# First attention's slots: GpSimd waits for the buffers of four slots at once, at every fourth slot, in place of at every slot

## What is computed

```python
feat = (x @ W).reshape(n_nodes, H, D)
e = leaky_relu(el[src] + er[dst], 0.2)
ex = exp(e - segment_max(e, dst)[dst])
denom = segment_sum(ex, dst)
out = segment_sum((ex / denom[dst])[:, :, None] * feat[src], dst)
```

## Time and profile before

| | |
|---|---|
| median of 3 runs | 3279.8 us |
| profiled execution: span from its first to its last instruction | 3272.4 us |
| PE busy | 2624.1 us, 80% |
| DVE busy | 2317.7 us, 71% |
| ACT busy | 1279.7 us, 39% |
| POOL busy | 1066.1 us, 33% |
| first attention's slots | about 1556 to 2793 us |

### The profile page before, as it was taken

One profiled execution on the slowest core, in us unless ns is written; L12 is line 12 of the kernel. 1 busy time (PEld: TensorE's weight loads), 2 busy tenths in 40 slices (PEclk: granted clock), 3 DMA queues, 4 the chain that ended last, 5 costly groups with the idle time before them and its releaser, 6 DMA issues.

```text
span 3272.4 us, 51000 instructions
## 1 busy us (share of the span) xinstructions
PE 2624.1 (80%) x17803; PEld 1952.4 (60%) x17803; DVE 2317.7 (71%) x3106; ACT 1279.7 (39%) x3089; POOL 1066.1 (33%) x1299
## 2 busy tenths in 40 slices
PE   5777777999899997285888888777677677876999
PEld 3666664545455554265777777555555555674888
DVE  7999997796334443288788787966666666785786
ACT  7888884020001112001444444444544454503443
POOL 3000000111102225530566666666666665003000
PEclk8999999999899998597999999899988999967999
DMA  4444446434477872031677766666666666061543
GB/s 134 183 181 177 167 182 240 123 113 134 143 262 255 261 253 89 15 106 53 181 194 193 198 190 184 179 186 186 184 184 189 184 184 190 12 200 54 158 155 112
DMA packets 316172, 537.23 MB, mean 164 GB/s; under 512 B 114066, under 2 KB 219044, under 8 KB 315668
## 3 DMA queue, kind: packets, MB, share of 16 engines
q1 hardware_dynamic: 244724, 308.43, 28.8%
q0 software_dynamic: 71200, 225.54, 24.7%
HBM read 419.84 MB, written 115.21 MB: 164 GB/s over the span
## 4 chain that ended last, share of the span: by engine, by line
PE 53%; DVE 28%; issue 7%; another core or an unknown queue 5%; ACT 5%; DMA 1%; POOL 1%; DVEq 0%; ACTq 0%; SPq 0%; POOLq 0%
PE ps L1718 20%; PE ps L1499 14%; PE ps L1706 8%; DVE a L590 8%; PE ps L1635 4%; DVE a L585 3%; DVE a L586 3%; PE ps L1405 2%; DVE a L1165 2%; DVE a L836 2%; ACT oht L1370 2%; DVE a L862 1%; ACT oh L1372 1%; PE ps L1633 1%
## 5 line engine op out<-in xcount | busy, mean ns | idle before, releaser
L1718 PE MATMUL ps<-a,oh 128*128 128x260 f32 x2008 | 508.8, 408 | 133.2 <-DVE a L1177 55.1
L1827 POOL DMA_INDIRECT a<-t,mid x502 | 486.7, 969 | 376.9 <-PE ps L1718 140.3
L1370 ACT ACTIVATE oht<-iota,mid 128x128 f32<-128x128 f32 x830 | 333.3, 402 | 627.0 <-PE ps L1718 396.4
L1499 PE MATMUL ps<-a 128*128 128x512 f32 x1200 | 555.4, 602 | 13.4 <-DVE a L769 13.4
L1718 PEld LDWEIGHTS ps<-a,oh 128*128 128x128 f32 x2008 | 389.7, 201 | 233.7 <-ACT oh L1372 97.3
L1165 DVE TENSOR_TENSOR a<-a,ps 128x520 f32 x415 | 286.3, 690 | 290.3 <-PE ps L1718 193.5
L1718 PE MATMUL ps<-wts,oh 128*128 128x260 f32 x1312 | 342.8, 416 | 115.2 <-DVE wts L1177 42.7
L1466 PE MATMUL ps<-a 128*128 128x200 bf16 x1568 | 320.4, 255 | 108.7 <-issue 51.1
L1827 POOL DMA_INDIRECT wts<-t,mid x328 | 313.5, 956 | 178.8 <-issue 82.9
L1718 PEld LDWEIGHTS ps<-wts,oh 128*128 128x128 f32 x1312 | 261.4, 206 | 184.4 <-ACT oh L1372 77.6
L1499 PEld LDWEIGHTS ps<-a 128*128 128x128 f32 x1200 | 218.8, 192 | 221.8 <-issue 215.4
(11 more groups left out here) (329 smaller groups left out, 3910.5 us busy)
## 6 DMA issues: line engine op xcount, KB each, us to landing
a<-at_d SPq DMA_DIRECT2D x60, 1280.0 KB, 6.1
at_d<-a SPq DMA_DIRECT2D x49, 800.0 KB, 3.3
mt_d<-a SPq DMA_DIRECT2D x49, 800.0 KB, 4.9
a<-mt_d SPq DMA_DIRECT2D x30, 1280.0 KB, 6.1
a<-trlo_d SPq DMA_DIRECT2D x49, 512.0 KB
ot_d<-a SPq DMA_DIRECT2D x49, 320.0 KB, 5.9
a<-ot_d SPq DMA_DIRECT2D x49, 256.0 KB, 3.3
a<-t,mid POOLq DMA_INDIRECT x502
```

The lines of the kernel that those rows point to most:

```text
L1370: e.activation(oht[:, k, :], iota[:, :], ACT.Abs, bias=ndl[:, k, s:s + 1]).then_inc(*own.inc())
L1499: m = e.matmul(acc[f].rearrange("p (x d) -> p x d", x=8), X[:, hi, P * f:P * (f + 1)], a, start=(hi == 0), stop=end, skip_group_check=True)
L1718: t = e.matmul(pbig[b][:, 512 * u:512 * u + 260], oh[:, so, k, :], hrows[2 * r + k][:, 260 * u:260 * (u + 1)], start=(k == 0), stop=(k == 1))
L1827: e.indirect_dma_start(out=hrows[2 * r + k], out_offset=None, in_=t2, in_offset=bass.IndirectOffsetOnAxis(ap=srci[:, k, s:s + 1], axis=0)) ...
```

## The change

GpSimd's wait moves from every slot to every fourth (s = 10, 14, 18, ...), and it then asks for the buffers of all four slots that follow: `head_mm` at s - 6 in place of s - 9. The last group's wait is cut at 405. The three slots behind it have no wait of their own.

The two waits of the first stage on a register's value change in form: the value goes through a register operation (the larger of it and 1) into a register that is kept, in place of `e.snap`.

```diff
@@ scalar @@
             ereg = [e.alloc_register(f"ae{i}") for i in range(4)]
+            ends = e.alloc_register("pair_end")
             e.wait_ge(*V("regs"))
...
-                e.wait_ge(slot_done, e.snap(ereg[p % 4], min_val=1, max_val=S))
+                e.reg_alu(ends, ereg[p % 4], 1, ALU.max)
+                e.wait_ge(slot_done, ends)
@@ tensor @@
             breg, freg = [], []
+            free = e.alloc_register("free_at")
...
-                    e.wait_ge(window_free, e.snap(freg[s // 8 % 4], donate=True, min_val=1, max_val=NPAIR + 8))
+                    e.reg_alu(free, freg[s // 8 % 4], 1, ALU.max)
+                    e.wait_ge(window_free, free)
@@ gpsimd @@
             def gather_heads(s):
                 r = s % NR
-                if s >= NR:
-                    e.wait_ge(head_mm, s - NR + 1)
+                if s >= NR and (s - NR) % 4 == 0:
+                    e.wait_ge(head_mm, min(s - NR + 4, NS - NR))
                 for k in range(2):
```

## The result

The changed kernel took 3413.03 us (median of 4 runs, 3398.04 to 3420.16); the kernel before took 3279.59 us beside it (3279.08 to 3279.99). The ratio is 1.040, 95% interval 1.037 to 1.043: slower by 133 us, where 50 were forecast. The profiled span went from 3272.4 to 3406.9 us, 134.5 more.

A forecast was written before the change was run, and what follows sets the result against it. While gathers are under way, their DMA queue was taken to hold back TensorE's counts, so the engines wait in rounds. Terms of 12 + 38 + 0 + 0 = 50 us gave 3330 us, range 3257 to 3392.

The forecast's parts named there:

- the register operations: First stage, two register waits: VectorE hides the added operations, 0 us; 17 us were that cover gone.
- the two kinds of round in the first part: First stretch, 1605 to 2047 us: rounds of eight gathers take 11.94 or 14.54 us, half of each assumed.
- the last part's single rounds: Last stretch, 2108 to 2763 us: a round of eight gathers takes 11.94 us, 2.985 per slot against 2.931.
- the sum of the last stretch: 2108 to 2763 us, 223.5 slots: the fourth count adds 0.2 us per round, 12 us; ends 1 and 114.
- the first stretch: 1605 to 2047 us, 145 slots: 3.31 us per slot against 3.048, 38 us; ends -9 and +85.
- The long round: First stretch: the fourth slot is computed only after the release, 11.74 + 2.8 = 14.54 us, 3.635 per slot.
- the upper end: First stretch: TensorE's clock falling from 0.98 to 0.91 costs 30 us at most, left out of the sum.
- what the DMA queue needs for the gathers: Long stretches of the first attention: the queue's draining, about 1.47 us per gather, sets the round and delays TensorE's counts.
- Much slower (3400 us): Rival: first stretch +85, clock +30 (part within that), last stretch 35, together 120 to 150 us; chance 0.16.
- Longer rounds save the stops: Rival, not slower, 3262 us: first stretch -16 us, last stretch a small gain, -2 us; chance 0.20.
- Rounds of eight below 11.5 us: Sign in the trace after: rounds of eight gathers ending before 11.5 us would show the forecast wrong.
- No difference: Rival, 3283 us: first stretch finds its four counts (-9), last pays for the fourth (+12), +3 us; chance 0.14.

The follow-up runs named there:

- e1: The changed kernel with GpSimd's wait put back before every slot, the register operations kept: 3281.43 us, ratio 1.002 to the kernel before.
- e9: The changed kernel itself, unaltered, run on another chip where the kernel before took 2976 us: ratio 1.0031 to it.
- e3: The changed kernel with waits at every slot and half of each gather's bytes (half rows): 3278.81 us, ratio 1.0013 to the kernel before.
- e4: The changed kernel, waits still in groups of four, with half of each gather's bytes (half rows): 3389.47 us, ratio 1.035 to the kernel before.
- e15: The changed kernel's groups of four plus a wait for the landing of the previous group's last gather: ratio 1.109 to the kernel before.
- e14: The changed kernel with waits at every slot and a memset of one column behind each gather: ratio 1.0007 to the kernel before.
- e18: The changed kernel with waits in groups of two slots in place of four: 3313.07 us, ratio 1.011 to the kernel before.

## Why the prediction was wrong

**Right:** slower, GpSimd's waits fewer and longer, ended by the last of four counts; rows still in time (3.6 us idle ahead of L1177); the first stage unchanged (VectorE 397.05 against 397.09 us of 400, and ScalarE's last clearing of PSUM starts at 529.2 us, before at 531.5), with the register operations put at 0 and 7.6 us in e1; the two kinds of round in the first part; the last part's single rounds, 11.8 us against 11.94 forecast. That the long and the short rounds of the first part come half and half was taken for want of a row, and was luck. One reading was loose without harm: VectorE is the gathered rows' first reader, but TensorE reads them too, scaled.

**The step that failed** is the sum of the last stretch, "every round becomes one of eight, and ends with the fourth count". Eight rounds were of sixteen, and two pairs nearly so. The forecast let TensorE finish four slots in a round of eight gathers; counted in the trace it finished five (180 slots done at 2186.52, 185 at 2198.41, 190 at 2208.40). So surplus counts pile up until the next group's wait is met at once; GpSimd then issues 20 us without a stop, and for the second half of it nobody gets a count. The ten double rounds take 285 us for 80 slots, 3.56 each against 2.93: 50 us, where the whole term was 12. The 36 single rounds together cost 2. The forecast held the length of a burst fixed by the code; it is fixed only from below.

**A term too small:** the first stretch, 38 forecast, 66 measured. The long round was put at 14.54 us, from one catch-up of 2.8 us; the long rounds take 15.7 on average and up to 18.5. The slot after the release also waits for ScalarE's and VectorE's work and runs at the low clock: 3.80 us for eight matmuls at 1883.94 in the changed kernel, where 1.84 were assumed. I gave the clock to the upper end only; at 0.84 in the last part and 0.94 in the first it belonged in the sum. How much it adds by itself, no run separates.

**A term left out:** the slots ahead of the first part, 16 us. The sum has nothing for them, and the first wait alone, which asks for three slots more, idles 9.3 us longer; on the other kind of chip it is the greater part of what the change costs (8.1 us in e9).

**A mechanism that was wrong:** that the round is "what the DMA queue needs for the gathers". e3 and e4 refute it as far as bytes go. The Trainium skill (DMA: Bandwidth & Descriptors, on the anatomy of a GpSimd-issued DMA) was set aside in the forecast because the rounds contradict it; by its 2.0 us plus bytes over 436 GB/s a gather's bytes move in less than the 1.25 us of its issue, and slots would come at 2.5 us; both are estimates. e9's trace, on the other kind of chip, shows just those 2.50 us. e15 shows a landing later than the rule's 2.6 us for 266 KB, 3.44 us behind the issue's end (the row at 2405.38), with seven other gathers just ahead of it. On the chip of the result something else held the slots.

A sign of that something was visible in the trace of the kernel before, outside the stretch I read. Between 1285 and 1365 us GpSimd issues 64 small gathers (4 KB each), one each 1.25 us, 3 GB/s in all. TensorE's work of that time does not wait for them. Stretches of the kernel before, then TensorE's instructions and one of VectorE's there:

```profile
1320.00:1340.00 20.00, 2.03 (x7) 0.73 (x7) 0.99 (x1) 0.00 (x0) 15.13 (x17) 0.50 0.08 3
...
1380.00:1400.00 20.00, 18.24 (x196) 16.20 (x194) 20.00 (x24) 0.00 (x0) 0.00 (x0) 1.00 0.18 50
```

```profile
1361.62 0.33 PE L1633 MATMUL ps<-small,yt 100*128 100x200 bf16 x1 [2.47 <-issue]
1364.42 0.33 PE L1635 MATMUL ps<-tbl,yt 128*128 128x200 bf16 x1 [2.47 <-issue]
...
1372.12 0.32 PE L1635 MATMUL ps<-tbl,yt 128*128 128x200 bf16 x1 [0.38 <-issue]
...
1372.84 0.99 DVE L862 TENSOR_REDUCE a<-ps 128x32 f32<-128x800 f32 x1 [36.81 <-remote]
```

A matmul comes each 2.80 us while TensorE waits for nothing the profile shows, and VectorE stands for 36.81 us; 7 us after the last of these gathers the matmuls follow one another 0.7 us apart, and the stretch from 1380 has 196 of them. From 1320 to 1340 seven matmuls are done. The same 20 us in e14, on the other kind of chip, with the same line of gathers going out, though 14 in place of 17 (about 1.4 us apart):

```profile
1320.00:1340.00 20.00, 19.11 (x210) 17.97 (x211) 19.36 (x28) 0.00 (x0) 15.85 (x14) 1.00 0.25 61
```

210 matmuls. In these 20 us all eight traces from chips of the first kind have 7 or 8 matmuls, and all twelve from the second kind 210 to 213. So on the first kind TensorE itself is slowed during a long burst of gathers, not only the news of its counts, and the bytes are next to nothing. It starts some 7 us into the burst (its first gather is at 1284.91): at 1291 us the matmuls still follow each other without a gap. That the gathers are the cause is read from this timing; no run took them away. Had I read this stretch, I would have priced a burst longer than eight gathers as time in which TensorE does little, and asked whether groups of four can ever run together.

**The rivals.** "Much slower (3400 us)" came nearest. Its first stretch (+85) and last (+35) add up to 120 against the 119 measured in these two, but 66 and 53 each, and the last by bursts of sixteen, not by a later fourth count; the total is near by luck. "Longer rounds save the stops" fails. Rounds of eight below 11.5 us, which the forecast named as a sign that it is wrong, are there (six of 11.0 to 11.1, and the two of 10.3 ahead of a pause of 0.6), but each is followed by a longer one (12.4, and 17.4 and 16.1). "No difference" holds on the chips of the second kind, for another reason: there GpSimd hardly stops. In e9 it waits for a slot nine times in 1605 to 2047, 18.5 us in all, and never in the last part.

**Open:** what in the chips differs, and whether it is the chip or a passing condition of it (five sets, each on another chip, and the executions of a kernel in a set agreed but for the one of 3913 us); whether the number of rows or GpSimd's issuing itself slows the others, since the runs with half the rows met only chips of the second kind; by which way it slows them: a TensorE that gets its instructions late would look as it does at 1350 us, and the queue q14 of instructions moves one packet from 1300 to 1360, which neither shows nor excludes it; and how the first part's 27 us in e18 come about.

## What to carry to other kernels

A wait for a group of buffers asks for the last of several counts and lets the issuer run longer without a stop; both have a price only if the issuer's run disturbs those it waits for, so look in the trace for any place where it already runs long, even with tiny transfers, and read what the other engines do there. When waits are grouped, ask how far surplus counts can let two groups run together, and price the first wait, which nothing hid here. And measure on more than one chip before a tuned order is kept: what loses 4 % on one lost 0.3 % on another.

## What the runs showed of the hardware

- The same kernel takes 3274 to 3280 us on some chips and 2976 to 2979 on others. The first stage is the same on both: in 100 to 500 us VectorE is busy for 397.05 us in the changed kernel's profile and for 397.05 in e9's. Most of the difference lies where GpSimd issues gathers: the last gather of the slots starts at 2774.0 us in the kernel before and at 2508.3 in e14, 266 us of the 292 between their spans.
- On the slower kind gaps between TensorE's instructions begin once GpSimd has issued 4 KB gathers for some 7 us without a stop, at 3 GB/s, and later they come 1.4 us apart (a matmul with its weight load 2.80 us). In a burst of sixteen no count of slots is seen for up to 12 us; bursts of twelve in e18 cost nothing. Half the bytes change nothing (ratio 1.0013). In e9, on the other kind, gathers come each 1.25 us without a stop, and VectorE idles 5.5 us in all ahead of its 415 additions.
- The issue of the 4 KB gathers takes longer where TensorE is not disturbed. Line L1834 of the kernel before, and the same gathers in e14:

```profile
L1834 POOL DMA_INDIRECT a<-el_d,src_f x64 | 60.5, 945 | 21.0 <-issue 19.2 <-DVE bcol L872 1.8
```

```profile
L1844 POOL DMA_INDIRECT a<-el_d,src_f x64 | 78.3, 1223 | 21.0 <-issue 19.2 <-DVE bcol L874 1.8
```

- A memset of one column (0.11 us) behind each gather fits into the gap of 0.30 us and costs nothing that can be told (1.0004 and 1.0007, both on the second kind).
